# A macaron block with mixture of experts: q and k strips copied by DMA and rounded by GpSimd, in place of zero-one products and ScalarE copies

## The chip, the cores and the metric

The kernel runs on one core of one Trainium2 chip. The metric is the device time of one execution in microseconds; the median of several executions is compared. Lower is better.

## The reference

`x` holds 8 x 256 tokens of width 128. The block is, in this order,

```
x = x + 0.5 * ffn(layernorm(x))      # round 0
x = x + retention(layernorm(x))
x = x + 0.5 * ffn(layernorm(x))      # round 1, the same weights

def ffn(x):
    h = layernorm(x, g, b)
    q, k, v = split(h @ w_qkv + b_qkv)            # 16 heads of 8 columns
    x = x + softmax(q k^T / sqrt(8)) v @ w_o + b_o
    h = layernorm(x, g2, b2)
    top-2 of 8 experts by h @ gate_w, softmax over the two
    return x + sum of the two experts' relu(h W1 + b1) W2 + b2, weighted
```

The retention has 8 heads with rotary q and k, a decay in place of a softmax, a norm per head and a silu gate. All is float32.

## The kernel before, in words

The 2048 tokens are handled in 4 chunks of 512 per round, so `n` is 0 to 3 in round 0 and 4 to 7 in round 1. A round has three stages: the attention of the chunks (0 to about 150 us, and 513 to about 661), the experts over pages of sorted tokens, and, between the rounds, the retention.

Attention. q and k come out of one product each as 128 columns x 512 tokens, with the heads' columns along the partitions. The score products need a head's 8 columns of q or k split in three terms (high times high, high times low, low times high), in a strip of 32 partitions, with one more row for the maximum, and four such strips fill the 128 partitions: group `g` of `GA` = 4 holds four heads. Both parts are float32r, a rounded float32: ScalarE rounds the projection to `hi` (`high_part`, L1316), VectorE makes `low`, the rest (`low_part`, L772). TensorE then brings the rows to their places with matrices `sel` that hold only zeros and ones (`PeFfn.spread`, L1585: one product with `hi`, one with `low`, 128x128x512, for each of q and k and each `g`), and ScalarE evacuates the result from PSUM into the strips `qp` and `kp` (`ActFfn.strip`, L1323), adding the constant row. That is 8 spreads, 16 products and 8 strips for each chunk.

The steps. A chunk has 8 steps (two sequences x four groups). In step `s` VectorE adds the transposed maxima to q (`qm`, L879), divides the results of an earlier step (`weigh`, L781 and L783) and takes the maxima of the next step's scores (`biggest`, L790, two of 128x1024); TensorE transposes the maxima (L1592), makes the next step's scores (L1610) and this step's transposed scores in two halves (L1627), and the value products of the step before (L1646); ScalarE takes the two exponentials (L1400) and evacuates results (L1336). Each engine has its own order written out in its `steps`; the waits on semaphores tie them. The next step's scores of a chunk's last step, 7, are the first scores of the following chunk.

Beside its own steps a chunk carries two other chains: the projections of the next chunk `new` (transposed rows in step 0, q in step 2, k in step 4, v in step 7, all through PSUM bank 5) and the tail of the chunk before, `old` (merge in step 1, output projection in 3, second norm in 4 and 5, logits in 6, routing in 7). The spreads of `new` stand in steps 3 to 6, two in each (`SPREAD`), in PSUM banks 0 and 1 after the maxima have left them:

```
SPREAD = {3: ((0, 0), (0, 1)), 4: ((0, 2), (0, 3)), 5: ((1, 0), (1, 1)), 6: ((1, 2), (1, 3))}
```

and TensorE waits for their evacuation before the next step's scores. The first chunk of a round has no chunk ahead of it: chunk 0 has its spreads in `head`, chunk 4 in `opened`, at the end of the retention. So in each round three chunks of four are spread within steps.

SyncE issues nearly all DMAs, in program order: the loads, the fill of the routing pages `xs` with blanks (L535, 10.9 MB from DRAM to DRAM), the page loads of the experts, the half-swaps for the rotary (`swap`, L503), and again the expert weights (L514) when the retention is done. GpSimd has the norm roots, `xn`, the routing weights and the scatters to the pages in the attention, and is otherwise free there.

Of the kernel before, what the change touches and what calls it, by code (L numbers as in the profile page):

```python
# [28 lines left out]
AUG = 24  # L29
# [22 lines left out]
def constants(NT):  # L52
# [9 lines left out]
    for h in range(HR):  # L62
# [13 lines left out]
    blank[:, D] = 4 * NT * P + np.arange(XPAGES * P)  # L76
    sums = np.concatenate([np.arange(P)[:, None] < np.arange(P)[None, :], np.ones((P, P), bool)], 1)
# [4 lines left out]
        "c_tok": tok.reshape(P, -1).astype(np.uint32), "c_blank": blank,  # L82
# [31 lines left out]
def build(nc, a, out):  # L114
# [6 lines left out]
    with ctx:  # L121
# [3 lines left out]
        def sg(name, per):  # L125
# [85 lines left out]
        qp = sb("qp", [P, 2, GA, CH], F32R)  # L211
        kp = sb("kp", [P, 2, GA, CH], F32R)
# [58 lines left out]
            stat=8, rstd=1, rstd_x=1, xn=4, z=4, xnb=1, hTp=1, hT=1, qkp=2, hi=2, low=2, spread=8, strip_q=4, strip_k=4, vps=1, vaug=1,  # L271
            s_ps=16, smax=16, mTp=8, qm=8, st_ps=16, pexp=16, pv=8, ou=8, oqp=8, rec=8, o_tm=8, oTp=1, oT=1,
            x1p=1, x1=1, stat2=8, rstd2=1, z2=5, h2Tp=1, h2n=1, lgp=1, lg=1, top=4, tix=4, dv=2, ev=1, gw=4, one=2, taken=1, cum=4,
            half=1, x1c=4, x_done=4, chain=2, chain2=1).items()}
        m = {k: sg("m_" + k, v) for k, v in dict(
# [111 lines left out]
        SPREAD = {3: ((0, 0), (0, 1)), 4: ((0, 2), (0, 3)), 5: ((1, 0), (1, 1)), 6: ((1, 2), (1, 3))}  # L387
# [65 lines left out]
        class SpMoe:  # L453
# [62 lines left out]

        @block.sync
        def _(e):
# [16 lines left out]
            e.dma_start(xs_d.rearrange("(p j) d -> p (j d)", p=P), a["c_blank"].rearrange("(p j) d -> p (j d)", p=P)).then_inc(ld["blank"], 16)  # L535
# [7 lines left out]
            load_experts(e)  # L543
            SpMoe.experts(e, 1)
# [9 lines left out]
        class PoolFfn:  # L554
            @staticmethod
            def selections(e, rnd):
# [4 lines left out]
                for k, part, i in ((0, 0, 0), (0, 0, 1), (0, 1, 2), (1, 0, 0), (1, 0, 2), (1, 1, 1)):  # L561
                    e.tensor_copy(sel[:, k, part, :, :].rearrange("p g (j i d) -> p g j i d", i=4, d=DK)[:, :, :, i, :], columns).then_inc(picks.sem, 1)
# [35 lines left out]
            def steps(e, n):  # L598
# [150 lines left out]
        class DveFfn:  # L749
# [1311 lines left out]
```

## Time and profile before

| what | us |
|---|---|
| three runs | 794.21, 796.71, 797.71; median 796.71 |
| the profiled execution | 793.33, span 791.5 |
| busy: TensorE, VectorE, ScalarE, GpSimd | 668.6, 535.8, 479.8, 356.8 |
| chain that ended last | TensorE 56%, VectorE 14%, ScalarE 12%, waits for nothing seen 7% |

The span runs from the first instruction to the last, the time of the execution is a little longer. Busy time is summed over an engine's instructions, and engines work side by side. In the profile every line is that of the kernel file, PE is TensorE, DVE VectorE, ACT ScalarE, POOL GpSimd, and SPq the queue from which SyncE issues DMAs. The rows below give, for some steps, how long each engine was busy in a window, and what it waited for.

### The profile page before, as it was taken

To read this page: it belongs to the slowest core of one execution; us is meant where nothing else is said; L and a number is where in the kernel's file an instruction comes from. 1 tells how busy PE (TensorE), PEld (TensorE's weight loads), DVE (VectorE), ACT (ScalarE), POOL (GpSimd) and SP (SyncE) were. 2 spreads that over 40 slices of the span, in tenths; PEclk is the share of its full clock that TensorE was granted. 3 is DMA by queue.
4 is the path that set the end of the run, shared out by engine and by line. 5 is a ranking of instruction groups with operands and counts; after the bars stand their busy time and mean duration, and the time that the engine had idled before them with its cause. 6 is when DMAs were issued, how large, how long until landed. Compare 5 with 4: busy or idle time off the path is not lost.

```text
span 791.5 us, 17975 instructions
## 1 busy us (share of the span) xinstructions
PE 668.6 (84%) x5632; PEld 523.9 (66%) x5632; DVE 535.8 (68%) x1565; ACT 479.8 (61%) x1043; POOL 356.8 (45%) x493
## 2 busy tenths in 40 slices
PE   5899999777679949899999997889999877849991
PEld 3555555445679938699988996745555544749990
DVE  3879788853525437988988885687978884533333
ACT  3677677643358835566665655477777653526774
POOL 6501122735535550767667676640130464363541
PEclk9899999977979979999999998999999987878996
DMA  8990000013222133122220220060000002022215
GB/s 282 397 329 5 2 1 17 31 38 126 71 68 70 46 101 80 55 54 56 55 54 10 47 54 2 1 241 2 1 2 1 28 31 57 30 73 71 69 38 170
DMA packets 32108, 56.67 MB, mean 72 GB/s; under 512 B 5744, under 2 KB 23024, under 8 KB 31568
## 3 DMA queue, kind: packets, MB, share of 16 engines
q1 hardware_dynamic: 27472, 45.67, 19.1%
q0 software_dynamic: 4544, 9.84, 3.7%
q8 instruction: 49, 0.80, 0.4%
q14 instruction: 43, 0.35, 0.1%
HBM read 36.22 MB, written 22.01 MB: 74 GB/s over the span
## 4 chain that ended last, share of the span: by engine, by line
PE 56%; DVE 14%; ACT 12%; issue 7%; another core or an unknown queue 4%; DMA 3%; POOL 2%; SPq 1%; DVEq 0%; POOLq 0%; ACTq 0%
PE ps L1882 8%; PE ps L1897 8%; PE ps L1646 6%; ACT pt L1400 5%; PE ps L1979 5%; PE ps L1627 4%; DVE msp L790 4%; PE ps L2000 3%; PE ps L1585 3%; PE ps L1950 2%; PE ps L1984 2%; PE ps L2013 2%; PE ps L1573 2%; PE ps L2015 1%
## 5 line engine op out<-in xcount | busy, mean ns | idle before, releaser
L1400 ACT ACTIVATE pt<-ps 128x1024 f32<-128x1024 f32 x128 | 131.0, 1024 | 63.3 <-PE ps L1627 59.3
L790 DVE TENSOR_REDUCE msp<-ps 128x4 f32<-128x1024 f32 x128 | 150.3, 1217 | 0.4 <-PE ps L1610 0.3
L1465 ACT ACTIVATE hid<-ps,ws 128x128 f32<-128x128 f32 x312 | 89.1, 370 | 55.8 <-PE ps L1882 21.1
L663 POOL DMA_INDIRECT os<-osb,xt x78 | 75.6, 969 | 82.5 <-DVE osb L1122 74.8
L1897 PE MATMUL ps<-wpack,hid 128*128 x624 | 88.6, 288 | 13.5 <-ACT hid L1465 13.3
L655 POOL DMA_INDIRECT xs<-rows,sidx x64 | 62.8, 981 | 77.4 <-issue 27.1
L1882 PE MATMUL ps<-hTe,ws 128*128 128x128 f32 x624 | 88.6, 288 | 10.5 <-ACT hTe L1456 6.1
L1897 PEld LDWEIGHTS ps<-wpack,hid 128*128 128x128 f32 x624 | 80.7, 202 | 15.5 <-issue 15.4
L1882 PEld LDWEIGHTS ps<-hTe,ws 128*128 128x128 f32 x624 | 81.5, 204 | 11.2 <-ACT hTe L1456 6.6
L1627 PE MATMUL ps<-qm,kp 32*128 32x256 f32 x512 | 67.1, 339 | 21.4 <-ACT pt L1400 12.7
L1627 PEld LDWEIGHTS ps<-qm,kp 32*128 32x128 f32 x512 | 40.8, 193 | 59.0 <-ACT pt L1400 39.3
L1646 PE MATMUL ps<-pt,vaug 128*32 128x256 f32 x1024 | 74.8, 415 | 0.0
L1122 DVE TENSOR_TENSOR osb<-ps,wpack 128x128 f32<-128x128 f32 x78 | 22.7, 290 | 68.3 <-PE ps L1897 41.0
L1113 DVE COPY ws<-wpack 128x516 f32 x78 | 34.9, 447 | 38.7 <-issue 34.3
L1527 ACT ACTIVATE oh<-ps,ors 128x128 f32<-128x128 f32 x128 | 40.0, 366 | 34.6 <-POOL ors L710 34.3
L879 DVE TENSOR_TENSOR qm<-ps,qp 128x256 fp32r<-128x256 f32 x64 | 26.9, 421 | 40.1 <-PE ps L1592 33.7
L710 POOL TENSOR_TENSOR ors<-ors,mhalf 128x2 f32<-128x2 f32 x64 | 47.4, 741 | 11.7 <-POOL ors L707 11.7
L717 POOL TENSOR_TENSOR yT<-on,sg 128x256 f32<-128x256 f32 x64 | 51.3, 801 | 1.1 <-ACT on L1534 1.1
L1456 ACT ACTIVATE hTe<-ps,vec 128x128 f32<-128x128 f32 x78 | 36.4, 470 | 24.0 <-remote 13.2
L707 POOL TENSOR_SCALAR ors<-omv 128x2 f32<-128x2 f32 x64 | 19.5, 305 | 66.7 <-issue 46.7
L1646 PEld LDWEIGHTS ps<-pt,vaug 128*32 128x32 f32 x1024 | 28.6, 115 | 29.7 <-issue 16.3
L1336 ACT ACTIVATE ou<-ps 128x256 f32<-128x256 f32 x64 | 24.6, 384 | 38.2 <-PE ps L1646 32.9
(196 smaller groups left out, 1562.3 us busy)
## 6 DMA issues: line engine op xcount, KB each, us to landing
xs<-in_c_blank SPq DMA_DIRECT2D x1, 10872.0 KB, 44.1
wpack<-in_wmoe SPq DMA_DIRECT2D x2, 4112.0 KB, 13.6
xt<-xs SPq DMA_DIRECT2D x78, 72.0 KB
swap<-qr SPq DMA_DIRECT2D x32, 128.0 KB, 2.3
swap<-kr SPq DMA_DIRECT2D x32, 128.0 KB, 2.3
rows<-os SPq DMA_DIRECT2D x8, 256.0 KB, 3.4
xt<-os SPq DMA_DIRECT2D x8, 256.0 KB, 5.0
decay<-in_c_decay SPq DMA_DIRECT2D x1, 1536.0 KB, 10.8
```

What stands on the lines that cost most here:

```text
L655: e.indirect_dma_start(xs_d, bass.IndirectOffsetOnAxis(ap=sidx[:, n % 2, k, i:i + 1], axis=0), rows[:, n % 2, k, i, :].bitcast(U32), None) ...
L663: e.indirect_dma_start(os_d, bass.IndirectOffsetOnAxis(ap=xt[:, k % XRING, D:D + 1].bitcast(U32), axis=0), osb[:, k % 8, :], None).then_in ...
L710: e.tensor_tensor(ors[:, b, 1, :], ors[:, b, 0, :], mhalf[:, 0:2], ALU.pow).then_inc(r["ors"].sem, 1)
L717: e.tensor_tensor(yT[:, bb, h, :], on[:, u % 2, :], sgT[bb][:, h, :], ALU.mult).then_inc(r["yT"].sem, 1)
L790: e.tensor_reduce(msp[:, s % 2, :, 64 * pr + AUG:64 * pr + AUG + 33:32].rearrange("p q j -> p j q"), ps[:, score_banks(2 * s + pr), :].rea ...
L1400: e.activation(pt[:, u % 4, :, :], ps[:, 2:4, :], ACT.Exp, scale=float(DK) ** -0.5).then_inc(f["pexp"].sem, 1)
L1465: e.activation(hid[:, t % 2, i, :], ps[:, t % 2, i * P:(i + 1) * P], ACT.Relu, bias=ws[:, k % 4, WB1 + i:WB1 + i + 1]).then_inc(m["hid"].s ...
L1527: e.activation(oh[:, b, q, :], ps[:, 2 + b, q * P:(q + 1) * P], ACT.Identity, scale=ors[:, b, 1, q:q + 1]).then_inc(r["oh"].sem, 1)
L1627: last = e.matmul(ps[:, 2 + jj, q * SEQ:(q + 1) * SEQ], kp[j:j + 32, n % 2, g, lo + q * P:lo + (q + 1) * P], qm[j:j + 32, s % 2, :], start ...
L1646: last = e.matmul(ps[32 * j:32 * j + 32, result_bank(n, s), 0:SEQ], vaug[:, n % 2, at:at + 32], pt[:, (2 * s + j // 2) % 4, j % 2, k * SEQ ...
L1882: last = e.matmul(ps[:, t % 2, i * P:(i + 1) * P], ws[:, k % 4, i * P:(i + 1) * P], hTe[:, t % 2, :], start=True, stop=True)
L1897: last = e.matmul(ps[:, 2 + t % 2, 0:D], hid[:, t % 2, i, :], wpack[:, bass.ds(x, 1), WW2 + i * D:WW2 + (i + 1) * D].rearrange("p o w -> p ...
```

## The change

For the three chunks of a round that are not its first, the strips are no longer made by TensorE and ScalarE. SyncE copies rows of `hi` and `low` from SBUF to SBUF (`deal`): `COPIES` names, for q and k, the part (0 is `hi`, 1 is `low`) and its places in a strip; each copy has 32 partitions x 512 columns. The partitions of a strip are ordered anew for it: place `i` of column `d` is partition 4 d + i, and the fourth place is left to the augmented row (`AUG` is 3 and no longer 24). That row comes from a constant in DRAM, two transfers of 32 partitions x 2048. As a copy by DMA keeps the bits, and the products want float32r, GpSimd then copies each strip onto itself (`qs` and `qp` are the same memory, once as float32 and once as float32r). The order of the queues: SyncE issues the transfers of chunk 1 between the two halves of the blank fill, those of chunks 2 and 3 before the page loads, and those of 5 to 7 after the reload of the expert weights; GpSimd rounds the next chunk's strips after the second norm of the chunk before. `SPREAD`, its products, strips and waits are gone from `steps`. The first chunk of a round keeps its spreads, with the new partition order.

```
-AUG = 24
+AUG = 3
...
-        qp = sb("qp", [P, 2, GA, CH], F32R)
-        kp = sb("kp", [P, 2, GA, CH], F32R)
+        strips = ExitStack()
+        qp = strips.enter_context(nc.sbuf_tensor("qp", [P, 2, GA, CH], F32R))
+        kp = strips.enter_context(nc.sbuf_tensor("kp", [P, 2, GA, CH], F32R))
+        strips.close()
+        qs = sb("qs", [P, 2, GA, CH])
+        ks = sb("ks", [P, 2, GA, CH])
...
-        SPREAD = {3: ((0, 0), (0, 1)), 4: ((0, 2), (0, 3)), 5: ((1, 0), (1, 1)), 6: ((1, 2), (1, 3))}
+        COPIES = ((0, (0, 1)), (1, (2,))), ((0, (0, 2)), (1, (1,)))
...
+        def dealt_to(n):
+
+            return n - n // NCH - 1
...
+        def deal(e, n):
+
+            b = n % 2
+            if n % NCH >= 2:
+                e.wait_ge(f["st_ps"].sem, f["st_ps"](n - 2, 16))
+                e.wait_ge(f["qm"].sem, f["qm"](n - 2, 8))
+            for k in range(2):
+                e.dma_start((qs, ks)[k][AUG::4, b, :, :].rearrange("p g t -> p (g t)"), a["c_aug"][k]).then_inc(dealt[k].sem, 16)
+            for k in range(2):
+                e.wait_ge(f["hi"].sem, f["hi"](n, k + 1))
+                for part, places in COPIES[k]:
+                    if part:
+                        e.wait_ge(f["low"].sem, f["low"](n, k + 1))
+                    for i in places:
+                        for g in range(GA):
+                            e.dma_start((qs, ks)[k][i::4, b, g, :], (hi, low)[part][g::4, k, :].bitcast(F32)).then_inc(dealt[k].sem, 16)
...
-            e.dma_start(xs_d.rearrange("(p j) d -> p (j d)", p=P), a["c_blank"].rearrange("(p j) d -> p (j d)", p=P)).then_inc(ld["blank"], 16)
+            fill_blank(e, 0)
+            deal(e, 1)
+            fill_blank(e, 1)
+            for n in range(2, NCH):
+                deal(e, n)
             SpMoe.experts(e, 0)
...
             load_experts(e)
+            for n in range(NCH + 1, 2 * NCH):
+                deal(e, n)
             SpMoe.experts(e, 1)
...
          class PoolFfn:
...
             def steps(e, n):
...
                 if not opens(n):
                     PoolFfn.rstd(e, n - 1)
+                if not closes(n):
+                    PoolFfn.rounded(e, n + 1, 0)
+                    PoolFfn.rounded(e, n + 1, 1)
...
+            def rounded(e, n, k):
+
+                e.wait_ge(dealt[k].sem, dealt[k](dealt_to(n) + 1, 0))
+                for g in range(GA):
+                    e.tensor_copy((qp, kp)[k][:, n % 2, g, :], (qs, ks)[k][:, n % 2, g, :]).then_inc(strip_ready[k].sem, 1)
...
         class PeFfn:
...
             def scores(e, n, s):
...
+                if not opens(n) and s < GA:
+                    for k in range(2):
+                        e.wait_ge(strip_ready[k].sem, strip_ready[k](dealt_to(n), s + 1))
...
-                    if new is not None:
-                        for i, (k, g) in enumerate(SPREAD.get(s, ())):
-                            ActFfn.strip(e, new, GA * k + g, k, g, i)
...
-                    if new is not None and s in SPREAD:
-                        e.wait_ge(f["smax"].sem, f["smax"](ahead[0], 2 * ahead[1] + 1))
-                        for i, (k, g) in enumerate(SPREAD[s]):
-                            e.wait_ge(f["low"].sem, f["low"](new, k + 1))
-                            PeFfn.spread(e, new, k, g, i)
```

`hi` and `low` of a chunk may be written again only when the copies of the chunk before have landed, so `high_part` and `low_part` wait for that.

## Rows read from the trace of the kernel before

**Rows 1.** Groups by line and shape: busy us, mean ns, idle time before them.
```profile
L1585 PE MATMUL ps<-hi,sel 128*128 128x512 f32 x64 | 29.1, 455 | 0.8 <-DVE low L772 0.8
```

**Rows 2.** Timeline of VectorE, chunk 0: start us, us, instruction, idle before, releaser.
```profile
44.65 0.42 DVE L879 TENSOR_TENSOR qm<-ps,qp 128x256 fp32r<-128x256 f32 x1 [1.46 <-PE ps L1592]
...
45.36 2.35 DVE L790 TENSOR_REDUCE msp<-ps 128x4 f32<-128x1024 f32 x2
49.08 0.42 DVE L879 TENSOR_TENSOR qm<-ps,qp 128x256 fp32r<-128x256 f32 x1 [1.37 <-PE ps L1592]
```

**Rows 3.** Timeline of TensorE, the same step.
```profile
47.04 0.50 PE L1585 MATMUL ps<-hi,sel 128*128 128x512 f32 x1
...
48.17 0.50 PE L1627 MATMUL ps<-qm,kp 32*128 32x256 f32 x4
48.60 0.44 PE L1592 MATMUL ps<-ident,msp 128*128 128x128 f32 x2
...
50.05 0.50 PE L1627 MATMUL ps<-qm,kp 32*128 32x256 f32 x4 [0.34 <-ACT pt L1400]
```

**Rows 4.** Timeline of ScalarE, chunk 0, steps 4 and 5.
```profile
41.72 0.69 ACT L1316 ACTIVATE hi<-ps,vec 128x512 fp32r<-128x512 f32 x1
...
47.81 1.27 ACT L1323 ACTIVATE kp<-ps,vec 128x512 fp32r<-128x512 f32 x2 [0.25 <-PE ps L1585]
```

**Rows 5.** Windows: start and end, length, busy us of each engine, granted clock, DMA.
```profile
35.12:57.91 22.79, 21.05 (x206) 12.34 (x199) 15.88 (x27) 17.40 (x25) 2.39 (x3) 1.00 1.01 327
39.16:44.65 5.49, 5.14 (x44) 2.70 (x42) 3.78 (x7) 4.28 (x7) 0.00 (x0) 1.00 1.09 338
70.41:75.53 5.12, 4.76 (x48) 3.10 (x41) 4.82 (x15) 2.67 (x5) 0.04 (x1) 1.00 0.00 0
75.53:81.03 5.50, 5.15 (x44) 2.70 (x42) 5.16 (x12) 4.29 (x8) 1.16 (x2) 1.00 0.00 1
81.03:86.05 5.02, 4.68 (x46) 2.83 (x44) 3.62 (x7) 4.18 (x7) 0.00 (x0) 1.00 0.01 3
86.05:93.04 6.99, 6.65 (x50) 4.03 (x48) 4.39 (x20) 3.80 (x6) 0.00 (x0) 0.76 0.00 1
575.97:581.39 5.42, 5.08 (x50) 3.37 (x48) 4.39 (x20) 3.58 (x6) 0.00 (x0) 1.00 0.02 5
125.11:131.00 5.89, 5.54 (x54) 3.82 (x52) 4.89 (x24) 3.59 (x7) 1.10 (x1) 1.00 0.00 0
```

**Rows 6.** Timeline of the DMA issues of SyncE's queue.
```profile
6.75 1.04 SPq L529 DMA_DIRECT2D sums<-in_c_sums  x1
...
9.86 7.52 SPq L531 DMA_DIRECT2D rwo<-in_rwo  x1
17.42 0.45 SPq L532 DMA_DIRECT2D decay<-in_c_decay  x1
...
18.71 0.43 SPq L534 DMA_DIRECT2D sin<-in_c_sin  x1
19.18 0.63 SPq L535 DMA_DIRECT2D xs<-in_c_blank  x1
...
299.97 2.49 SPq L503 DMA_DIRECT2D swap<-qr  x4
```

**Rows 7.** DMA issues by tile: KB each, median us from issue to landing.
```profile
xs<-in_c_blank SPq DMA_DIRECT2D x1, 10872.0 KB, 44.1
...
swap<-qr SPq DMA_DIRECT2D x32, 128.0 KB, 2.3
...
sin<-in_c_sin SPq DMA_DIRECT2D x1, 128.0 KB, 10.2
```

**Rows 8.** Window in which only the loads fill the queue; last number GB/s.
```profile
16.00:20.00 4.00, 3.53 (x21) 2.19 (x19) 3.23 (x12) 2.59 (x5) 2.98 (x5) 1.00 1.03 418
```

**Rows 9.** Groups by line and shape on GpSimd.
```profile
L612 POOL TENSOR_TENSOR xn<-xn,bo_bc 128x512 f32<-128x512 f32 x8 | 10.2, 1273 | 1.5 <-POOL xn L609 1.5
...
L562 POOL CAST sel<-ident 128x128 fp32r<-128x128 f32 x12 | 4.3, 399 | 0.1
```

**Rows 10.** Instructions of one tile or line: ns minimum, median and maximum.
```profile
L790 DVE TENSOR_REDUCE msp<-ps x128: 1193/1217/1227, 19.1 to 656.9; 128x4 f32<-128x1024 f32 x128
...
L1242 DVE TENSOR_TENSOR swap<-swap,sin x32: 678/685/1218, 304.4 to 470.0; 128x512 f32<-128x512 f32 x32
```

More of the change, by code:

```diff
@@ L81, in constants @@
         "c_route": np.tile(route, (P, 1)), "c_sums": sums.astype(np.float32),
-        "c_tok": tok.reshape(P, -1).astype(np.uint32), "c_blank": blank,
+        "c_tok": tok.reshape(P, -1).astype(np.uint32), "c_blank": blank, "c_aug": aug,
     }
@@ L270, in build @@
         f = {k: sg("f_" + k, v) for k, v in dict(
[L271 removed]
+            stat=8, rstd=1, rstd_x=1, xn=4, z=4, xnb=1, hTp=1, hT=1, qkp=2, hi=2, low=2, vps=1, vaug=1,
             s_ps=16, smax=16, mTp=8, qm=8, st_ps=16, pexp=16, pv=8, ou=8, oqp=8, rec=8, o_tm=8, oTp=1, oT=1,
@@ L515, in load_experts, with fill_blank @@
             e.dma_start(wpack[:, :, WB2:], a["L0_ffn_b2"].partition_broadcast(P)).then_inc(ld["moe"], 16)
+        def deal(e, n):
[13 more added lines that the diff above has]
+                            e.dma_start((qs, ks)[k][i::4, b, g, :], (hi, low)[part][g::4, k, :].bitcast(F32)).then_inc(dealt[k].sem, 16)
+        def fill_blank(e, part):
+            lines = slice(part * P // 2, (part + 1) * P // 2)
+            e.dma_start(xs_d.rearrange("(p j) d -> p (j d)", p=P)[lines, :], a["c_blank"].rearrange("(p j) d -> p (j d)", p=P)[lines, :]).then_inc(ld["blank"], 16)
         @block.sync
@@ L561, in selections @@
                 for k, part, i in ((0, 0, 0), (0, 0, 1), (0, 1, 2), (1, 0, 0), (1, 0, 2), (1, 1, 1)):
-                    e.tensor_copy(sel[:, k, part, :, :].rearrange("p g (j i d) -> p g j i d", i=4, d=DK)[:, :, :, i, :], columns).then_inc(picks.sem, 1)
+                    e.tensor_copy(sel[:, k, part, :, :].rearrange("p g (j d i) -> p g j d i", i=4, d=DK)[:, :, :, :, i], columns).then_inc(picks.sem, 1)
             @staticmethod
@@ L646, in scatter @@
                 if n == 0:
-                    e.wait_ge(ld["blank"], 16)
+                    e.wait_ge(ld["blank"], 32)
                     e.wait_ge(zeroed.sem, 5)
@@ L1585, in spread @@
                     last = e.matmul(ps[:, bank, :], sel[:, k, part, g, :], src[:, k, :], start=(part == 0), stop=(part == 1))
-                last.then_inc(f["spread"].sem, 1)
+                last.then_inc(spread_done.sem, 1)
             @staticmethod
@@ L1602, in scores @@
                 if opens(n) and s < GA:
-                    e.wait_ge(f["strip_q"].sem, f["strip_q"](n, s + 1))
-                    e.wait_ge(f["strip_k"].sem, f["strip_k"](n, s + 1))
+                    for k in range(2):
+                        e.wait_ge(strip_done[k].sem, strip_done[k](n // NCH, s + 1))
+                if not opens(n) and s < GA:
+                    for k in range(2):
+                        e.wait_ge(strip_ready[k].sem, strip_ready[k](dealt_to(n), s + 1))
                 wait_earlier(e, f["smax"], n, 2 * s)
@@ L1714, in opened @@
                     e.wait_ge(r["sc"].sem, r["sc"](s - 1, 2 * HR))
-                    e.wait_ge(f["strip_q"].sem, f["strip_q"](n, GA))
-                    e.wait_ge(f["strip_k"].sem, f["strip_k"](n, GA))
+                    for k in range(2):
+                        e.wait_ge(strip_done[k].sem, strip_done[k](n // NCH, GA))
                     PeFfn.scores(e, n, 0)
@@ L1810, in steps @@
                         PeFfn.out_t(e, *two_back(n, s))
-                    if new is not None and s - 1 in SPREAD:
-                        k, g = SPREAD[s - 1][1]
-                        evacuated = (f["strip_q"], f["strip_k"])[k]
-                        e.wait_ge(evacuated.sem, evacuated(new, g + 1))
                     if ahead:
@@ L1817, in steps @@
                     if opens(n) and s == 0:
-                        e.wait_ge(f["strip_q"].sem, f["strip_q"](n, GA))
-                        e.wait_ge(f["strip_k"].sem, f["strip_k"](n, GA))
+                        for k in range(2):
+                            e.wait_ge(strip_done[k].sem, strip_done[k](n // NCH, GA))
                     last = closes(n) and s == 7
```

37 lines of the change are left out of this document (23 added, 14 removed).

## The prediction, made before the change was run

> **What bounds the kernel now.** I began with the busy shares of the page: TensorE is busy for 84% of the span, but its part of the chain that ended last is only 56%, with VectorE and ScalarE beside it, so no engine paces the whole. The change touches one stage, the macaron attention, so I looked at what ends each of its steps. A step runs from one `qm` of VectorE to the next. The plain step that starts at 44.65 us takes 4.43 us [rows 2]; VectorE is through with it (`qm`, the two small merges, both maxima) at 47.71 and then stands idle for 1.37 us until TensorE's transposed maxima arrive. TensorE is the one that is late: between the value products and the second half of the transposed scores it runs four spreads, from 47.04 to 48.17, that is 1.13 us, and only then turns the maxima (48.60) [rows 3]. ScalarE evacuates those spreads for 1.27 us and so starts its second exponential late; TensorE waits 0.34 us for it at 50.05 [rows 3, 4]. So in these steps one loop paces: values, spreads, strips on ScalarE, exponential, next scores. Step windows tell where this holds [rows 5]: in 81.03:86.05 VectorE is busy for 3.62 of 5.02 us, in 125.11:131.00 for 4.89 of 5.89; but in 70.41:75.53 for 4.82 of 5.12 and in 75.53:81.03 for 5.16 of 5.50, where VectorE itself is the bound.
>
> **What is removed, and what it gives.** Three of four chunks per round, six in all, lose 8 spreads of two products each and 8 strips (48 of the 64 hi products, mean 455 ns, as many low ones, and 48 strips of some 0.65 us) [rows 1, 4]. Busy time is not what is saved; each step falls to what is late next. That is VectorE's loop: 0.71 us from `qm` to the first maximum, 2.35 for the two, some 0.1 to start the turn, 0.48 from the turn to the next `qm` (48.60 to 49.08) [rows 2, 3]: 3.65 us. The loop of TensorE and ScalarE without spreads is shorter: 4.43 less 1.13 less 0.34 is 3.0.
> Chunk 0 (chunk 4 has the same pattern): steps 5 and 6, 4.43 to 3.65 each, give 1.56. Step 4, 5.49 us, has the k projection; its chain projection, `hi`, `low`, turn stays and needs about 4.4, so it gives 1.1. Steps 3 and 7 share the rest of the window, 22.79 - 5.49 - 8.86 = 8.44 [rows 5]; I put 3.65 and, with the value projection of about 0.4 more than the loop hides, 4.05: 0.74. Together 3.4, twice 6.8.
> Chunk 1: step 3 gives 0.1 and step 4 0.2 (VectorE is full); step 5, 5.02 to about 3.8, gives 1.2; step 6 lasts 6.99 us because the granted clock was 0.76 in it, that is, partly at 1.2 GHz, and goes to 4.7 by VectorE's 4.39 busy: 2.3. Chunk 5 has the same steps, with 5.42 instead of 6.99: 2.2 in all. Chunks 2 and 6: 0.1, 0.2, 1.2, and 5.89 to 5.05: 2.35 each [rows 5].
> Sum: 6.8 + 3.8 + 2.2 + 4.7 = 17.5 us.
>
> **What is added on SyncE's queue and the DMA.** Per chunk 2 transfers for the augmented rows and 24 of 64 KB, all issued by SyncE, one after another. The nearest row is the swap of the retention, also from SBUF to SBUF over 32 partitions: four issues in 2.49 us, 0.62 each [rows 6], landing 2.3 us after the issue begins [rows 7]. Ends for one issue: 0.45, as for the decay table, and 1.04, the dearest one that was not held [rows 6]. I take 0.62, the same kind of transfer.
> The long path is k: `hi` of k ends 3.25 us into step 4 (42.41 against 39.16) [rows 4, 5], 2.9 once ScalarE is not held up. Then 12 issues, 7.4 us; the last one lands 1.7 after its issue ends; then GpSimd rounds four strips, and TensorE needs the first of them when it computes the next chunk's first scores, at the start of step 7.
>
> **What is added on GpSimd.** Eight copies of 128x512 per chunk. No row has one. From below, a cast of 128x128 takes 399 ns, and four times the columns can't take less; from above, four such casts, 1.60 us; a two-input operation of 128x512 takes 1.27 [rows 9]. I take 0.9, since one input is less than two. GpSimd stands idle through steps 3 to 6 but for a few small operations [rows 5], so 7.2 us of it are hidden; behind the waiting copies on its queue stand the routing weights of the chunk before (wanted only after step 7), the next chunk's `xn` (wanted three steps into that chunk) and, in chunk 2, the first scatters, which start up to 3 us later and end about 1 us later; nobody waits for those before the closing chunk has ended.
> The Trainium skill, "GPSIMD Engine Reference", section "3.1 Elementwise — side-by-side cycle accounting", gives 769 ns for 512 elements in a tight loop and calls VectorE about twice as fast for ordinary elementwise work, which speaks against rounding on GpSimd. By that figure the copies are 0.13 us cheaper each than I took; no row shows the operation.
>
> **The wait that comes in place.** k[0] is ready 2.9 + 7.4 + 1.7 + 0.9 = 12.9 us into step 4. In chunks 0 and 4 the first scores are due at 4.4 + 3.65 + 3.65 + 0.1 = 11.8: 1.1 us of wait. In the other four chunks steps 4 to 6 last 5.3 + 3.8 + 4.7 = 13.8, or 14.1: no wait, with about 1 us to spare.
> In chunk 0 a second queue matters. The transfers of one queue go in order, and the first half of the blank pages now stands before the copies. The whole fill lands 44.1 us after 19.18, at 63.3; what stands before it (`sin`, issued at 18.71) lands 10.2 us later, at 28.9 [rows 6, 7]. So half of it moves by 46.1. Behind it queue the augmented rows and the twelve q strips, 1.3 MB, which at the 418 GB/s of 16:20 [rows 8] land at 49.2. Rounding q to 52.8, then k[0] at 53.7, against a slot at 50.6: a wait of 3.1. The second half of the fill lands before 75 us, long before the first scatter near 130.
> Sum: 17.5 - 3.1 - 1.1 = 13.3 us. The profiled execution is 793.33 us (span 791.5 and 1.8 around it); it becomes 780.0. The median of the three runs, 796.71, lies 3.4 above the profiled one, so I forecast 783.4.
>
> **Rivals.**
> A, GpSimd is the dear part. With 1.60 us a copy, q in chunk 0 is done at 55.6 and k[0] at 57.2 (3.5 worse), in chunk 4 0.7 worse, elsewhere 12.9 grows to 13.6 and still fits; and VectorE may be held up while GpSimd copies. The row that speaks for it: `swap*sin`, with two inputs in SBUF, takes 685 ns in the median and up to 1218 beside GpSimd; against it: the maxima, which read PSUM, stay between 1193 and 1227 all along [rows 10]. In these steps only the halved residual and some tiny operations are of the first kind: at most 0.5 us in each of six chunks. Together 3.5 + 0.7 + 3 = 7.2: 790.6.
> On this the Trainium skill, "SBUF — State Buffer", section "Who interferes with whom", says that a VectorE instruction with two SBUF inputs contends with a GpSimd one that reads SBUF, and that the port is locked for a whole instruction. By that rule the trace agrees on both kinds.
> B, a queue that is full. The issue of `rwo` was held for 7.52 us behind the expert weights [rows 6]. If the blank half holds SyncE in the same way until 46, q starts 13 us late, k follows it: 46.1 + 14.8 + 1.7 + 0.9 = 63.5 against 50.6, a wait of 12.9 in place of 3.1, so 793.2. Against it: the fill is few long packets, and its whole issue took SyncE no longer than others. In chunk 4 the same hold behind the expert weights would end about when `hi` of q exists, two steps on.
> C, slower: the k path is longer at every handover. Twelve serial issues multiply each error: with 1.04 us an issue the path is 5.0 us longer. The four chunks with 1 us to spare lose 4.0 each, chunk 4 loses 5.0 and chunk 0 3.0 (2 us of it lie under the queue's wait): 24 us more, so 807. It decides from an issue of about 0.89 us: with 3.2 more on the path these are 8.8, 3.2 and 1.2, the 13.3 of the gain. Against it: four swaps in a row average 0.62.
> D, nothing moves: VectorE fills each gap, or TensorE, with less to do, is granted the lower clock. The step 86.05:93.04 shows what that costs, 1.6 us over its twin of 5.42 [rows 5]; eight such steps would be needed to eat the gain, and the windows with 3.62 of 5.02 us of VectorE speak against the first: 796.
>
> **Chances.** My forecast (778 to 788) 0.58; better than 778, if no wait at all comes (17.5 gives 779, and cheaper issues or copies a little more) 0.09; A 0.11; B 0.06; D 0.07; C 0.09. The range for 8 in 10 is 776 to 793. Of 0.5%, 4 us, a measurement of this kernel can tell: faster by more than that is forecast, better, A and most of B, 0.82; the same 0.09; slower 0.09.
>
> **What would show it.** Right: plain steps 5 of chunks 0 and 4 near 3.65 us and paced by VectorE's maxima; no `ACT pt` wait after them; TensorE waiting 1 to 3 us for a GpSimd strip at step 7 of chunks 0 and 4 and nowhere else; SyncE issuing at about 0.6 us each; copies at 0.9. Wrong: steps that stay over 4 us (D), waits for GpSimd in chunks 1, 2, 5, 6 (C), SyncE held for many us before the q copies of chunk 1 (B), copies over 1.3 us (A).

## The result, and the profile after

The changed kernel takes 793.42 us in the median of 20 runs (787.77 to 800.77), the kernel before 797.71 us beside it (20 runs, 793.74 to 801.72). The ratio is 0.9958, with a 95% interval of 0.9938 to 0.9978: a gain of about 3.4 us where 13.3 were forecast. (The medians are 4.3 us apart; the ratio is not formed from them, and it leaves out the one execution, 800.77, in a slower state of the chip.) The profiled execution has a span of 790.4 us against 791.5. The first lines of the page after say that the work went where it was meant to go: against the page before TensorE is busy 5.6 us less, ScalarE 27.0 us less, GpSimd 29.4 us more. The mean granted clock is 0.896; it was 0.929.

```profile
span 790.4 us, 17936 instructions
...
PE 663.0 (84%) x5536; PEld 521.1 (66%) x5536; DVE 538.9 (68%) x1565; ACT 452.8 (57%) x995; POOL 386.2 (49%) x541
```

The windows of six steps answer to [rows 5] (columns as there: start and end, length, busy us of each engine, granted clock, DMA share, GB/s). They are a plain step of chunk 0, its step 7, steps 4, 5 and 6 of chunk 1, and step 7 of chunk 4.

```profile
48.02:51.61 3.59, 3.05 (x38) 1.76 (x36) 3.03 (x5) 2.44 (x4) 0.98 (x2) 1.00 0.50 180
51.61:60.06 8.45, 6.60 (x46) 4.45 (x44) 3.12 (x5) 2.73 (x5) 8.02 (x12) 0.60 0.94 337
77.21:83.22 6.01, 4.08 (x38) 2.06 (x38) 5.98 (x12) 3.12 (x4) 3.66 (x6) 1.00 0.25 95
83.22:88.22 5.00, 4.44 (x32) 2.55 (x32) 3.61 (x9) 2.55 (x4) 0.00 (x0) 0.66 0.26 99
88.22:93.51 5.29, 5.20 (x46) 3.36 (x44) 4.38 (x20) 2.68 (x4) 2.29 (x4) 0.72 0.05 14
538.58:547.65 9.07, 6.65 (x46) 4.54 (x44) 3.12 (x5) 2.77 (x5) 6.71 (x9) 0.64 0.06 19
```

The plain step has gone from 4.43 us to 3.59. The two steps 7 now last 8.45 and 9.07 us, twice a plain one, at a granted clock of 0.60 and 0.64. Step 4 of chunk 1 is 0.51 us longer than before, with VectorE busy in 5.98 of its 6.01 us; steps 5 and 6 behind it have a clock of 0.66 and 0.72, where step 5 had 1.00 before (and step 6 had 0.76).

TensorE's timeline at step 7 of chunk 0 (start us, us, instruction, in brackets idle time before it and what ended it):

```profile
51.14 0.44 PE L1645 MATMUL ps<-ident,msp 128*128 128x128 f32 x2 [0.43 <-DVE msp L844]
...
53.64 0.80 PE L1666 MATMUL ps<-kp,qp 32*128 32x256 f32 x8 [1.85 <-POOL qp L692]
54.21 0.66 PE L1683 MATMUL ps<-qm,kp 32*128 32x256 f32 x4
54.79 2.08 PE L1631 MATMUL ps<-wv,hT 128*128 128x128 f32 x8
56.80 1.94 PE L1702 MATMUL ps<-pt,vaug 128*32 128x256 f32 x16
```

The next chunk's first scores (L1666) wait 1.85 us for GpSimd's strips. That is a stall like the forecast one, and smaller than the 3.1 put there. But the value products behind it, 1.07 us for 16 at full clock (the same group at 49.02), now take 1.94: the granted clock is 0.52 from 53.64 to 60.06, that is, down at its lower level of 1.2 GHz for nearly all of what is left of the step. GpSimd's timeline and SyncE's issues beside it:

```profile
50.63 2.29 POOL L692 CAST qp<-qs 128x512 fp32r<-128x512 f32 x4 [18.06 <-DMA qs<-low]
52.92 2.30 POOL L692 CAST kp<-ks 128x512 fp32r<-128x512 f32 x4
55.21 3.15 POOL L651 TENSOR_SCALAR xn<-x_sb,mv,r 128x128 f32<-128x128 f32 x4
```
```profile
34.42 4.95 SPq L547 DMA_DIRECT2D qs<-hi  x8
39.42 2.56 SPq L547 DMA_DIRECT2D qs<-low  x4
43.06 5.22 SPq L547 DMA_DIRECT2D ks<-hi  x8
48.32 2.90 SPq L547 DMA_DIRECT2D ks<-low  x4
51.26 0.59 SPq L551 DMA_DIRECT2D xs<-in_c_blank  x1
...
511.65 0.62 SPq L529 DMA_DIRECT2D wpack<-in_wmoe  x1
...
513.02 9.17 SPq L539 DMA_DIRECT2D qs<-in_c_aug  x1
...
522.87 5.06 SPq L547 DMA_DIRECT2D qs<-hi  x8
527.98 3.28 SPq L547 DMA_DIRECT2D qs<-low  x4
531.30 5.25 SPq L547 DMA_DIRECT2D ks<-hi  x8
```

Four casts take 2.29 us, 0.57 each (a record of one lasts 0.62, and they overlap a little); I had put 0.9. An issue takes 0.62 us (4.95 for 8), as [rows 6] promised; over all 24 of a chunk it is 0.65 here and 0.67 in chunk 4. The last four lines are chunk 4: behind the expert weights the issue of the augmented rows is held for 9.17 us, the copies of q start 1.1 us after their `hi` was there (521.76), and those of k, queued behind them, 1.3 us after theirs (530.00 by ScalarE's timeline). VectorE, GpSimd and TensorE around the end of step 4 of chunk 1, one fence for each:

```profile
80.81 2.42 DVE L870 TENSOR_SCALAR rows<-x,mv,r 128x256 f32<-128x256 f32 x4
...
83.22 0.41 DVE L933 TENSOR_TENSOR qm<-ps,qp 128x256 fp32r<-128x256 f32 x1
```
```profile
80.62 2.46 POOL L692 CAST qp<-qs 128x512 fp32r<-128x512 f32 x4 [1.75 <-DMA qs<-low]
```
```profile
83.78 0.79 PE L1683 MATMUL ps<-qm,kp 32*128 32x256 f32 x4 [1.74 <-DVE qm L933]
```

The four `rows` operations (the normalised rows that are to be scattered) took 1.38 us together in the kernel before, from 79.49. They now take 2.42, and they lie beside the four casts of q, which take 2.46 us here and took 2.29 in chunk 0. `qm` stands behind them on VectorE's queue, TensorE stands idle for 1.74 us until it comes, and then runs at half clock. In chunk 2 TensorE stands idle for 1.98 us at the same place, and the step behind it keeps a clock of 1.00 and takes 3.63 us. All 24 `rows` operations by the view of one line (ns minimum, median and maximum); in the kernel before they were 395, 407 and 578:

```profile
L870 DVE TENSOR_SCALAR rows<-x,mv,r x24: 395/630/839, 80.8 to 684.5; 128x256 f32<-128x256 f32 x24
```

Steps 3 to 7 of the six changed chunks, summed from one `qm` to the next, were 150.1 us and are 148.9. That is the change of the span to 0.1 us. Outside these steps single stretches differ too (step 2 of chunk 0 is 1.64 us longer, the way from the last step of chunk 3 to chunk 4 1.20 shorter), but they cancel; so the 30 steps are where I looked.

### The profile page after: what moved, and what is told of

Its sections match the earlier page's. It is cut to its first block, busy times and chain, and to the rows that moved or that the text cites. A ratio compares the mean times of both kernels' runs of the same rounds, so it can differ in the third digit from the quotient of the medians.

```text
span 790.4 us, 17936 instructions
## 1 busy us (share of the span) xinstructions
PE 663.0 (84%) x5536; PEld 521.1 (66%) x5536; DVE 538.9 (68%) x1565; ACT 452.8 (57%) x995; POOL 386.2 (49%) x541
## 4 chain that ended last, share of the span: by engine, by line
PE 54%; DVE 21%; issue 6%; ACT 6%; DMA 4%; another core or an unknown queue 4%; POOL 3%; SPq 1%; DVEq 0%; POOLq 0%; ACTq 0%
PE ps L1927 8%; PE ps L1942 8%; DVE msp L844 8%; PE ps L2024 5%; PE ps L1702 5%; PE ps L1683 4%; PE ps L2045 3%; PE ps L1995 3%; PE ps L2029 2%; ACT pt L1456 2%; PE ps L2058 2%; DVE qm L933 2%; PE ps L1645 2%; PE ps L2060 2%
## 5 line engine op out<-in xcount | busy, mean ns | idle before, releaser
L1456 ACT ACTIVATE pt<-ps 128x1024 f32<-128x1024 f32 x128 | 131.1, 1024 | 83.2 <-PE ps L1683 80.6
L1683 PE MATMUL ps<-qm,kp 32*128 32x256 f32 x512 | 70.3, 353 | 22.0 <-DVE qm L933 17.3
L707 POOL DMA_INDIRECT xs<-rows,sidx x64 | 63.0, 985 | 49.2 <-ACT pt L1456 22.7
L1683 PEld LDWEIGHTS ps<-qm,kp 32*128 32x128 f32 x512 | 44.7, 208 | 63.0 <-ACT pt L1456 33.8
L1702 PE MATMUL ps<-pt,vaug 128*32 128x256 f32 x1024 | 83.1, 453 | 0.0
L1702 PEld LDWEIGHTS ps<-pt,vaug 128*32 128x32 f32 x1024 | 30.3, 123 | 34.5 <-issue 21.9
```

The costliest lines, as they stand in the source:

```text
L707: e.indirect_dma_start(xs_d, bass.IndirectOffsetOnAxis(ap=sidx[:, n % 2, k, i:i + 1], axis=0), rows[:, n % 2, k, i, :].bitcast(U32), None) ...
L1456: e.activation(pt[:, u % 4, :, :], ps[:, 2:4, :], ACT.Exp, scale=float(DK) ** -0.5).then_inc(f["pexp"].sem, 1)
L1683: last = e.matmul(ps[:, 2 + jj, q * SEQ:(q + 1) * SEQ], kp[j:j + 32, n % 2, g, lo + q * P:lo + (q + 1) * P], qm[j:j + 32, s % 2, :], start ...
L1702: last = e.matmul(ps[32 * j:32 * j + 32, result_bank(n, s), 0:SEQ], vaug[:, n % 2, at:at + 32], pt[:, (2 * s + j // 2) % 4, j % 2, k * SEQ ...
```

## The experiments

All ratios are to the kernel before on the same chip. There it took 740.6 us (runs 1 to 4, 11 runs of it), 797.3 us (runs 5 to 8, 17 runs) and 738.5 us (runs 9 and 10, 11 runs). The chips differ in stages that the change doesn't touch (last section); across chips I compare ratios and the lengths of steps only.

**1. The removal alone.** The output leaves out the placing of the new strips: strips of chunk 0 and 4 are used in their place.

```
-            deal(e, 1)                          (SyncE: all copies, chunks 1-3 and 5-7)
-                    PoolFfn.rounded(e, n + 1, 0)
-                    PoolFfn.rounded(e, n + 1, 1)
-    qp[j:j + 32, n % 2, g, ...], kp[j:j + 32, n % 2, g, ...]
+    qp[j:j + 32, 0, g, ...],     kp[j:j + 32, 0, g, ...]
```

> Only the removal is done: no copies by DMA, no rounding on GpSimd, no waits for them; every chunk reads the strips of its round's first chunk, so the new chunk's q and k reach the scores in none of six chunks (left out: the placing of its strips). The wait for the k strip in chunks 0 and 4 and the lengthened rows of VectorE must go under every theory. If the gain was lost to those two alone (wait and lock), the forecast sum without its waits stands: about 779 to 781 us, granted clock in the attention as before. If TensorE is granted the lower clock by itself once the spreads are gone, plain steps stay at 3.6 us but stretches at half clock appear in the attention with no wait ahead of them: 784 to 788 us.

Measured: 717.68 us, ratio 0.9695 (0.9667 to 0.9724); 22.9 us less. Step 7 of chunk 0 and step 4 of chunk 1, whose twins in the kernel after are 8.45 and 6.01:

```profile
50.53:54.53 4.00, 4.00 (x46) 2.73 (x44) 3.03 (x5) 2.52 (x5) 0.00 (x0) 1.00 0.79 261
71.82:76.79 4.97, 4.09 (x39) 2.06 (x38) 4.94 (x13) 3.12 (x4) 1.20 (x2) 1.00 0.01 2
```

Steps 3 to 7 of the six chunks sum to 131.1 us, 19.0 below the kernel before. The removal is worth at least what the prediction said (17.5): the medians give 22.9, and the ratio lies below both values that I had expected (779 us is 0.977 of 797). The clock is 1.00 in both steps shown. It isn't everywhere: step 5 of chunk 2 takes 4.90 us at a clock of 0.65 where its twins in chunks 1, 5 and 6 take 3.64, and steps 6 and 7 of chunk 6 take 6.05 and 5.12 at 0.67 and 0.72, so single steps fall to the lower clock even without an added stall.

**2. k[0] early.** The copies of group 0 go first and have a semaphore of their own; the blank pages go behind them. (Not shown: the augmented rows are split in the same way, and the copies of a round's third and fourth chunk wait for one more semaphore.)

```
-                for part, places in COPIES[k]:
-                    for i in places:
-                        for g in range(GA):
+                for g in range(GA):
+                    for part, places in COPIES[k]:
+                        for i in places:
                             e.dma_start(..., (hi, low)[part][g::4, k, :].bitcast(F32)).then_inc(dealt[k][min(g, 1)].sem, 16)
...
-            fill_blank(e, 0)
             deal(e, 1)
-            fill_blank(e, 1)
+            fill_blank(e, 0)
+            deal(e, 2)
+            fill_blank(e, 1)
```

> The copies of group 0 are issued first and have their own semaphore, and the blank fill stands behind the copies of chunks 1 and 2; all else as after the change. Theory of the wait: TensorE no longer waits at step 7 of chunks 0 and 4, these steps fall from 8.45 and 9.07 us to about 4.1, 9 us less: 784 to 786 us. Theory of the clock by itself: the two direct waits of 1.9 us go, but half clock stays elsewhere: 789 to 791. Theory of the lock: step 4 of chunks 1, 2, 5, 6 stays at 5.9 to 6.3 us.

Measured: 724.05 us, ratio 0.9793 (0.9762 to 0.9825), a little better than the 784 to 786 of 797 expected (0.983 to 0.986). Step 7 takes 4.0 us in both chunks; the stall is gone, and with it the lower clock. Steps 4 of chunks 1, 2, 5, 6 stay long at 5.66, 5.56, 5.13 and 5.65 (5.9 to 6.3 expected).

**3. The rounding late.** GpSimd rounds only when VectorE's `rows` of the step are through; nothing else is moved.

```
                 if not closes(n):
+                    if not opens(n):
+                        e.wait_ge(f["z2"].sem, f["z2"](n - 1, 5))
                     PoolFfn.rounded(e, n + 1, 0)
```

> GpSimd starts rounding q only after VectorE has written the normed rows of step 4, in chunks 1, 2, 5 and 6. Theory of the lock: the rows operation (630 ns in the median after the change, 407 before) is back at about 350 to 410, step 4 falls from 6.0 to 5.2 us, TensorE's idle time in it of 1.7 us to 1.0, and with it the half clock of steps 5 to 7 may go: 3 us directly, up to 7 with the clock: 786 to 790. If VectorE was not held by GpSimd, no change: 793.

Measured: 727.40 us, ratio 0.9838 (0.9807 to 0.9868), at the better end of what was expected (786 of 797 is 0.986). Windows of steps 4 and 5 of chunk 1, and of step 7 of chunks 0 and 4:

```profile
74.51:79.48 4.97, 4.09 (x38) 2.06 (x38) 4.93 (x13) 3.12 (x4) 1.20 (x2) 1.00 0.25 94
79.48:83.12 3.64, 2.96 (x32) 1.87 (x32) 3.61 (x9) 2.53 (x4) 2.29 (x4) 1.00 0.28 106
51.52:57.24 5.72, 3.85 (x46) 2.66 (x44) 3.12 (x6) 2.53 (x5) 5.70 (x10) 1.00 0.98 347
505.31:513.02 7.71, 5.26 (x46) 3.34 (x44) 3.12 (x6) 2.78 (x5) 5.61 (x9) 0.78 0.07 25
```

Steps 4 are 4.96 to 4.97 and steps 5 are 3.64 to 3.65 in all four chunks, the very lengths of the removal; the casts now lie in step 5 (2.29 us of GpSimd) and cost nothing there, beside the maxima, which read PSUM. So it was the meeting of `rows` and the casts, not GpSimd's work. The last two windows are a natural pair, of this execution with the changed kernel's: in chunk 0 TensorE waits 1.87 us at a clock of 1.00 and the step costs 1.7 us over the 4.0 of the removal; in chunk 4 it waits 2.45 us, the clock is 0.78, and the step costs 3.7. The first of them is nearly the stall of the changed kernel (1.85 us, and 4.45 in cost), without what came behind it. TensorE's timeline there:

```profile
53.57 0.51 PE L1668 MATMUL ps<-kp,qp 32*128 32x256 f32 x8 [1.87 <-POOL qp L694]
...
55.33 1.07 PE L1704 MATMUL ps<-pt,vaug 128*32 128x256 f32 x16
```

**4. Filler products that wait for the maxima.** Two unread 128x512 products ahead of the turn of the maxima, in steps 3 to 7.

```
+                    if not closes(n) and s >= 3:
+                        e.wait_ge(f["smax"].sem, f["smax"](ahead[0], 2 * ahead[1] + 1))
+                        for i in range(2):
+                            e.matmul(ps[:, 0, :], sel[:, 0, 0, i, :], hi[:, 0, :], start=True, stop=True)
```

> After the change, with two more products of 128x512 in steps 3 to 7 of the chunks that aren't a round's last, in place of TensorE's idle time before it turns the maxima; nobody reads them. Theory of the clock: TensorE stays at 2.4 GHz in more of the attention (the idle time in a plain step is 0.43 us, the two products take about 0.47), so steps 5 to 7 of chunks 1, 2, 5, 6 shorten: 787 to 790, the waits of chunks 0 and 4 unchanged. If work alone counts, it is 0 to 2 us slower: 793 to 796.

Measured: 731.47 us, ratio 0.9891 (0.9849 to 0.9932). That lies below the changed kernel's 0.9958 on its own chip (the intervals do not meet) and where the theory of the clock had it (787 to 790 of 797, 0.987 to 0.990); as the changed kernel was not run on this chip, I call it a sign and no more. Steps 7 of chunks 0 and 4 still take 7.90 and 8.09 us and step 4 of chunk 1 6.09, as expected: these products come ahead of the stall and the next ones after it, and TensorE's idle time before the waited scores is 2.00 us in chunk 0 (1.85 in the changed kernel).

**5. The changed kernel again**, unaltered, as the mark for runs 6 to 8 on their chip.

> The kernel after the change, unaltered, for its ratio and its steps on the chip of the runs beside it. The first four experiments ran where the kernel before took 740.6 us instead of 797, the difference lying in the expert stage; nothing in the change bears on that, so the ratio to before should stay near 0.996 (0.990 to 1.000), with steps 7 of chunks 0 and 4 above 8 us and step 4 of chunks 1, 2, 5 and 6 near 6.

Measured: 793.10 us (12 runs), ratio 0.9965 (0.9936 to 0.9994). Steps 7 are 7.54 and 9.05, steps 4 are 5.96, 5.63, 5.84, 5.85.

**6. Both remedies** (edits 2 and 3 together; the work is complete).

> Early k with the blank fill behind, and the late rounding, together. If wait and lock are what spoils the change, and the clock falls only behind them, the steps come to those of the removal alone (7 of chunks 0 and 4 at 4.0, 4 of the others at 4.97, 5 at 3.64): ratio 0.970 to 0.976, as the removal alone. If GpSimd or the copies cost something more, it stays above 0.980.

Measured: 776.91 us, ratio 0.9739 (0.9703 to 0.9776): 20.4 us below the kernel before, 16.2 below the change as it stands. Windows of step 7 of chunk 0 and of steps 4 and 5 of chunk 1:

```profile
51.41:55.42 4.01, 4.01 (x46) 2.73 (x44) 3.03 (x6) 2.54 (x5) 2.83 (x5) 1.00 0.75 254
72.71:77.67 4.96, 4.08 (x38) 2.06 (x38) 4.93 (x12) 3.12 (x4) 1.20 (x2) 1.00 0.26 94
77.67:82.61 4.94, 4.37 (x32) 2.55 (x32) 3.62 (x9) 2.69 (x4) 2.85 (x5) 0.65 0.25 95
```

Step 5 is 3.65 and 3.64 in chunks 2 and 6, but 4.94 and 4.87 in chunks 1 and 5, at a clock of 0.65 in the one shown. This is the best version that I ran with the work complete; steps 3 to 7 sum to 132.8 us.

**7. More work, stalls left.** The changed kernel with seven unread products ahead of the waiting scores in step 7 of chunks 0 and 4, and five in step 5 of chunks 1, 2, 5 and 6.

```
+                    fill = 7 if opens(n) and s == 7 else 5 if not opens(n) and not closes(n) and s == 5 else 0
+                    for i in range(fill):
+                        e.matmul(ps[:, 0, :], sel[:, 0, 0, i % GA, :], hi[:, 0, :], start=True, stop=True)
                     if ahead:
                         PeFfn.scores(e, *ahead)
```

> The kernel after the change with both stalls left as they are, and products that nobody reads put where TensorE stands idle in them: seven of 128x512 ahead of the waited-for scores at step 7 of chunks 0 and 4, five ahead of the scores of step 5 in chunks 1, 2, 5 and 6. Theory of the clock as a consequence: step 7 of chunks 0 and 4 falls from 8.5 or 9.1 us to about 6 (only the 1.9 us of the wait are left) and step 5 of chunks 1 and 5 from 5.0 to 3.7, while step 4 stays at 6.0: 5 to 8 us better than the control, ratio about 0.01 lower. If the loss is in the waits themselves, no gain: equal to the control or up to 2 us slower.

Measured: 781.37 us, ratio 0.9802 (0.9778 to 0.9826), 11.7 us faster than run 5 (5 to 8 expected) with 34 products more and nothing taken away; all five executions (781.05 to 782.90) lie below the fastest of the twelve of run 5 (786.95). Windows of step 7 of chunks 0 and 4 and step 5 of chunk 1, then TensorE's timeline in the first of them:

```profile
50.93:57.13 6.20, 5.48 (x53) 3.81 (x51) 3.12 (x5) 2.53 (x5) 6.20 (x11) 1.00 0.90 323
537.68:543.09 5.41, 5.41 (x53) 3.79 (x51) 3.12 (x5) 2.52 (x5) 4.53 (x7) 1.00 0.04 15
80.64:84.28 3.64, 2.96 (x32) 1.87 (x32) 3.61 (x8) 2.52 (x4) 0.00 (x0) 1.00 0.27 94
```
```profile
50.87 1.88 PE L1867 MATMUL ps<-hi,sel 128*128 128x512 f32 x7
53.47 0.51 PE L1666 MATMUL ps<-kp,qp 32*128 32x256 f32 x8 [0.72 <-POOL qp L692]
...
55.22 1.07 PE L1702 MATMUL ps<-pt,vaug 128*32 128x256 f32 x16
```

In chunk 0 the scores start 2.5 us into the step, no earlier than in the kernel after (2.0), so the wait for k is there in full. But the value products take 1.07 us again, and the step costs 2.2 us over the 4.0 of the removal where the changed kernel pays 4.45. In chunk 4 k[0] was ready some 1 us earlier in the step than in run 5 (1.5 against 2.5 us into it), and the products cover the wait. Steps 4 stay long (6.21, 6.15, 5.40, 5.65), yet all four steps 5 take 3.64 or 3.65; in run 5 those of chunks 1 and 5 took 5.04 and 4.99, those of chunks 2 and 6 3.64 as here. So the 11.7 us were not the length of the stalls themselves, but what followed them.

**8. Group 0 first, blank pages left in front.** Run 2's order of copies without moving the fill.

```
             fill_blank(e, 0)
             deal(e, 1)          (with the copies of group 0 first)
             fill_blank(e, 1)
```

> The copies of group 0 first, with their own semaphore, but the first half of the blank fill in front of the copies of chunk 1 as after the change, and q rounded wholly before k. If only the k copies are late, chunk 0 is cured like chunk 4: both steps 7 at 4.0. If the queue behind the blank fill counts in chunk 0, as forecast, q lands late there and its step 7 stays 1 to 2 us longer than chunk 4's; ratio 0.003 above the run with the fill moved.

Measured: 782.17 us, ratio 0.9833 (0.9800 to 0.9865). Step 7 takes 4.36 us in chunk 0 and 4.00 in chunk 4. GpSimd's timeline in chunk 0 has the first strip of q at 48.12 and k[0] at 51.57, ready at 52.19:

```profile
48.12 0.61 POOL L697 CAST qp<-qs 128x512 fp32r<-128x512 f32 x1 [15.41 <-DMA qs<-low]
...
51.57 0.62 POOL L697 CAST kp<-ks 128x512 fp32r<-128x512 f32 x1
```

So the blank pages in front hold the q strips back (the same cast of q, the first, comes at 37.8 in run 6), but once the first group doesn't wait for the other three this is worth 0.36 us where I expected 1 to 2. The order of the copies gave nearly all.

**9. Both remedies and filler** in steps 4, 5 and 6 of chunks 1, 2, 5 and 6, four products each.

```
+                    for i in range(4 if s in (4, 5, 6) and not opens(n) and not closes(n) else 0):
+                        e.matmul(ps[:, 0, :], sel[:, 0, 0, i % GA, :], hi[:, 0, :], start=True, stop=True)
```

> The version with the early k copies and the late rounding, with four unread 128x512 products ahead of the waited scores in steps 4, 5 and 6 of chunks 1, 2, 5 and 6. In that version step 5 still takes 4.94 and 4.87 us in chunks 1 and 5 against 3.65 and 3.64 in chunks 2 and 6. Theory (those two steps are lengthened by half clock that a short idle time of TensorE in step 4 brought): step 5 comes to 3.65 in all four chunks, steps 4 stay at 4.97, and about 2 to 4 us of the 777 are gained. Rival (the products lie on TensorE's own chain in these steps, or chunks 1 and 5 wait for something else): step 5 stays near 4.9 or every such step grows by up to 0.9 us, 777 to 788.

Measured: 722.53 us, ratio 0.9766 (0.9721 to 0.9811), so no gain over run 6's ratio, where 2 to 4 us were expected. Step 5 comes to 3.80 or 3.81 in all four chunks, near the 3.65 of the theory; but step 4 grows from 4.96 to 5.28 and step 6 to 5.90, 6.10, 5.50 and 6.10: windows of steps 4, 5 and 6 of chunk 1:

```profile
71.49:76.77 5.28, 4.89 (x45) 2.67 (x43) 5.03 (x13) 3.13 (x4) 1.20 (x2) 1.00 0.45 163
76.77:80.57 3.80, 3.52 (x43) 2.17 (x41) 3.70 (x9) 2.69 (x4) 2.85 (x5) 1.00 0.28 104
80.57:86.47 5.90, 5.23 (x58) 3.52 (x56) 4.86 (x22) 2.77 (x4) 1.74 (x3) 1.00 0.59 206
```

The clock is 1.00 in all three. Both sides were right in part: the filler keeps the clock, and where TensorE has no real gap it costs its own time.

**10. The removal again**, beside run 9.

> The removal alone once more (no copies, no rounding, no blank-page fill for the new strips; the output leaves out the placing of these strips), here on the same chip as the version with both edits. Theory (the early copies and the late rounding hide the whole placing by DMA and GpSimd but for single half-clock steps): 770 to 777 on a chip where the kernel before takes 797, ratio 0.967 to 0.975, so at most 5 us below the version with both edits. Rival (the transfers themselves, through contention in stages outside the attention, take several us): 760 to 768.

Measured: 718.94 us, ratio 0.9739 (0.9693 to 0.9785); 19.5 us less, with steps 3 to 7 at 127.8. The version with both remedies has the same ratio on its chip (intervals 0.9693 to 0.9785 and 0.9703 to 0.9776), and in run 1 the removal had 0.9695. In the profiles steps 3 to 7 are 132.8 us with both remedies against 131.1 and 127.8 in the two removals. So 0 to 5 us of the placing by DMA and GpSimd are left visible; from the intervals alone some 7 (run 10) or 9 (run 1) could hide. The chip was another than run 6's, so the comparison goes over the ratios.

**Steps at the lower clock.** The clock differs from execution to execution, and each profile is one. Of the 12 steps 5 to 7 of chunks 1, 2, 5 and 6, these had a granted clock under 0.9: 7 in the changed kernel, 6, 5 and 6 in runs 5, 2 and 8, where `rows` and the casts still meet; 1 and 3 in runs 3 and 6, where they don't; 1 each in runs 4, 7 and 9, with filler; 3 and 0 in the removal (runs 1 and 10); 1 in the kernel before.

## Why the prediction was wrong

The forecast was 783.4 us, and it came to 793.4: the size of the gain was wrong, the sign was right. Two steps of the prediction failed. It counted a stall of TensorE at its own length and put the clock behind it at nothing; and it took all of GpSimd's rounding in the four other chunks as hidden. In the profiled execution the 30 steps give this ledger, each entry a difference to the removal (run 1):

- removal 150.1 to 131.1: 19.0 gained
- step 7 of chunks 0 and 4, 17.5 against 8.0: 9.5 lost
- step 4 of chunks 1, 2, 5, 6, 24.1 against 19.9: 4.2 lost
- steps 5 to 7 of these chunks, 58.0 against 54.0: 4.0 lost
- what is left: 19.0 - 17.7 = 1.3, against a difference of 1.1 in the spans.

Each side is one execution. With run 10 as the removal, which had no step 5 to 7 at the lower clock, the gain is 22.3 and the loss in steps 5 to 7 is 7.3; the other two entries stay. So the split between those two lines is known to some 3 us, the rest to some tenths.

**The removal** was right in its mechanism and a little low in its size (17.5 for 19.0 and 22.3): plain steps 3.59 (3.65 foretold), step 4 of chunk 0 4.25 (4.4), steps 5 of chunks 1 and 2 3.64 where the clock stayed at 1.00 (3.8), step 6 4.54 (4.7). VectorE's loop of two maxima paces them. Steps 3 and 4 of chunks 1, 2, 5 and 6, put at 0.1 and 0.2 us since VectorE is full there, gave 0.32 and 0.53. The "four spreads" from 47.04 to 48.17 are four products, of two spreads; the 1.13 us are right.

**The costs added** were right or too high: 0.62 to 0.67 us an issue, landing after 2.3 and 1.9 us, 0.57 us a cast for 0.9. So rival A's price of a copy fell, and rival C: TensorE waits for a k strip only where it was foretold, in chunks 0 and 4. Rival B did not happen behind the blank half in chunk 0, but in chunk 4 it did, behind the expert weights: SyncE was held for 9.17 us. I had written that this hold "would end about when `hi` of q exists", and so it did, 0.4 us after; with the second transfer of augmented rows behind it, the copies of q began 1.1 us late.

**The wait in its place** was right as an idle time and wrong as a cost. In chunk 0, k[0] was ready at 53.5, as foretold (53.7), but by two errors that cancel: the q strips landed at 50.6 for 49.2, and rounding them took 2.3 us for 3.6. Its slot came at 51.8 in place of 50.6, so 1.85 us of waiting for 3.1; the slot was late since step 2 of this chunk, ahead of all that was forecast, took 6.46 us for the 4.82 of the kernel before, its value products 1.94 us for 1.07. In chunk 4 TensorE stood idle for 2.42 us, the 1.1 foretold and the 1.3 of the held queue. Together 4.27 us, and the prediction had 4.2; that the sums agree is luck. But step 7 of the two chunks cost 9.5. The sum counted a stall at its own length, and the other 5.2 us are what TensorE did behind it at the lower of its two clock levels. Run 7 shows it as cause and effect: with the wait left and the gap filled the clock stays at 1.00, and the two steps sum to 11.6 us in place of 17.5 (16.6 in run 5), though TensorE has 3.8 us more to do. (Of the gain in chunk 4 some 1 us belongs to the earlier strip.) A stall does not always bring the lower clock: that of 1.87 us in run 3 cost 1.7 us. I had read the lower clock in [rows 5] (0.76 in the step 86.05:93.04, 1.6 us) and took it only as rival D, as a price for having less work. Run 1 says that D holds for single steps (three of the 12 steps 5 to 7, together 3.3 us over those of run 10, which had none). The larger part came with the gaps that the change itself makes. The same row would have priced it, in hindsight: two stalls at 1.6 us make 3.2, for the 5.2 measured, and with the four late `qm`, which I had not foreseen, some 10.

**GpSimd's cover** failed in one place. "7.2 us of it are hidden" held for every step except step 4 of chunks 1, 2, 5 and 6, where the casts of q meet `rows`. Rival A had the mechanism, VectorE held up while GpSimd copies, but I looked for it among operations with two SBUF inputs and put at most 0.5 us a chunk, 3 in all; it cost 4.2 in step 4 alone. `rows` has one large input, `x`, and two columns of scalars. It takes 630 ns in the median where it took 407, up to 839. Run 3 takes the meeting away and nothing else: 405 ns in the median, step 4 back from 6.01 to 4.97, step 5 from 5.00 to 3.64. So the price was 1.04 us in VectorE's chain in chunk 1. What follows behind it is less sure. `qm` came late, TensorE stood idle for 1.74 us, and the clock fell: 1.36 us in step 5. But run 6, with the same cure, has 4.94 us there, and in chunk 2 step 5 keeps its 3.63 behind an idle time of 1.98. Only the counts speak for the link: 5 to 7 steps at the lower clock where `rows` and the casts meet, 1 and 3 where they don't.

The Trainium skill, "SBUF — State Buffer", section "Who interferes with whom", has more than the sentence on two inputs that I weighed: it lists `copy`, `cast` and `tensor_scalar` among the operations that can take the shared port in certain modes and then hold it, or wait for it, for a whole instruction. `rows` is a `tensor_scalar`, and this trace agrees in its direction: 1.04 us more for four beside four casts. That VectorE was in such a mode is not shown by any run here.

**What stays open.** Why the lower clock comes in one chunk and not in its twin: in run 6 TensorE stands idle for 0.70 us before `qm` of step 5 in chunk 1 and 0.69 in chunk 2, and the step is 4.94 in the one and 3.65 in the other; the changed kernel and run 3 are such a pair at step 7 of chunk 0 (1.85 and 1.87 us idle, 8.45 and 5.72 us long). Runs 7 and 9 showed only that keeping TensorE busy takes it away in step 5, in all four chunks. The 4.0 us of steps 5 to 7 are put down to the clock by the windows of chunk 1 (0.66 and 0.72) and by the counts above; step 6 and step 7 were not isolated, and how much of this the lighter steps bring by themselves (rival D) and how much the late `qm` was not separated. A version with fewer and larger copies was not tried.

## What to carry to other kernels

Price a new stall of TensorE at its length and at what the lower clock may take from the work behind it: here 1.85 us of idle time made a step 4.45 us longer, and in another execution 1.87 made it 1.7 longer. Place a piece of work that "hides" on an idle engine by what the neighbours do at that moment: the same four casts cost nothing beside reductions from PSUM and 1.04 us beside four `tensor_scalar` from SBUF. And when a group of transfers feeds a loop, let the first member be complete first and give it a semaphore of its own: changing that order, with the semaphore, took the ratio from 0.9965 to 0.9833.

## What the runs showed of the hardware

- A kernel became 11.7 us faster by 34 products that nobody reads (run 7), and the granted clock stayed at 1.00 in the two steps in which it had been 0.77 and 0.64 in run 5 (0.60 and 0.64 in the profile after).
- VectorE's `tensor_scalar` of 128x256 from SBUF went from 407 to 630 ns in the median, 839 at most, beside GpSimd's casts of 128x512; the maxima of 128x1024 from PSUM stayed as they were, 1216 for 1217. The casts themselves went from 616 to 667 ns in the median beside `rows` of chunk 1.
- GpSimd casts 128x512 from fp32 to the rounded form in 0.62 us (0.57 from one to the next), 128x128 in 0.40 [rows 9]: four times the columns for 1.5 times the time.
- A load of 4.1 MB in the queue held SyncE's next issue for 9.17 us; the half blank fill of 5.4 MB held none.
- The kernel before takes 797 us on one chip and 740 on another. By the traces of before (797) and of run 1 (740) most of that lies where the experts work: 341.8 against 317.9 us from the last step of chunk 3 (at 171 us) to chunk 4, with the retention in it, and some 132 against 108 from the last step of chunk 7 to the end. Why is open.
